# Where eight chunks of a scan pipeline do their side work, and where in the program VectorE's loop begins

## The chip, the cores and the metric

The kernel runs on one core of one Trainium2 chip. The time is that of the device, in microseconds (us), from the start to the end of one execution. All engines of the core take part: TensorE (PE in the profile; its weight loads are PEld), VectorE (DVE), ScalarE (ACT), GpSimd (POOL) and the DMA queue of SyncE (SP).

## The reference

Eight batches of 1024 rows of 256 numbers go through four residual stages: a Mamba-like selective scan (`attn_a`), a mixture of 16 experts with the top 6 chosen by a router (`ffn`), a linear attention (`attn_b`) and the mixture again. Only the first two stages are touched.

```python
def attn_a(x):                       # D_INNER 512, D_STATE 16
    xn = layernorm(x)
    x_in, z = split(xn @ in_proj)
    x_conv = silu(conv4(x_in));  Bm, Cm = split(x_conv @ x_proj)
    delta = clip(softplus(x_conv @ dt_proj), 1e-4, 10)
    for t in range(L):
        h = exp(clip(delta[t] * A, -10, 0)) * h + delta[t] * Bm[t] * x_conv[t]
        if t % 16 == 15: h = h * min(1, 10 / norm(h))
        y[t] = Cm[t] . h + D_param * x_conv[t]
    return layernorm(x + (y * silu(z)) @ out_proj)
def ffn(x):
    probs = softmax(x @ router_w + router_b); gate = top6 of probs / their sum
    return sum over e of (x @ expert_w[e]) * gate[:, e]
```

## The kernel before

A tile is 128 rows of one batch; there are 64. `step(i, k, stages)` is written once for every engine, and each engine runs its own copy for the tiles in turn; semaphores alone tie them together. In one step the scan works on tile i, the input side (normalization, projection, convolution, delta) on tiles i+1 to i+4, the output projection and its norm on tile i-1, the router on tile i-2 and the experts on tile i-3. Steps 4 to 59 are a hardware loop of 28 turns (`pipeline`, line 208), two tiles a turn (k = 0 and 1); the rest is written out.

A step has 8 chunks c of 16 rows, since the state norm is bounded every 16 rows. One chunk is a ring through four engines:

- VectorE: `scan` (L996) over 128 x 1088, two expert sums (L1078), `reduce` (L1004) of ScalarE's squares, `bound` (L1013, L1015), which scales the last column and so lets the next scan begin.
- ScalarE: squares of the last column (L438), the decays' exponentials of the next chunk (L432), the logarithm and exponential of the norm (L444, L447).
- GpSimd: `product` (L362) of chunk c-1 with C, then `inputs` (L370) of chunk c+1, which the scan of c+1 waits for. In some chunks an `extra` of one tile-wide product follows: u in chunk 1, z's gate sz (L383) in chunk 4, the convolution's output (L386) in chunk 5, the residual sum x1b (L390) in chunk 7.
- TensorE: per chunk one pair of experts (L738) and some of the projections.

Everything else is fitted between: VectorE's `start(c)` is scan and expert sums, `halfway(c)` the reduce, `end(c)` the bound. Work between halfway and end lies beside ScalarE's norm; the reduce has to wait for the squares. The 8 + 3 small steps of the router (`route_step`, `route_gate` with selp, L1068, and gate, L1070) and the output norm (o3, L1194; o4, L1197) stand there. ScalarE makes 64 decay forms zr (L423, each 128 x 128) for each tile, and the table DECAYS says how many in each chunk. In chunk 0 ScalarE makes xn (L526), which TensorE transposes (L781) ahead of `sum_states(3)` (L704). In chunk 1 TensorE turns the sums back (`sums_back`, L712), which VectorE's gating yg (L1157) waits for; the router's transposes (L720) and the input projection (L797) follow. `settle()` is a semaphore increment on VectorE and nothing else.

After tile 63 the attention and the second mixture follow, in the last third of the time.

Of the kernel before, what the change touches and what calls it, by code (L numbers as in the profile page):

```python
# [10 lines left out]
NTILES = NB * NT  # L11
# [13 lines left out]
DECAYS = (0, 6, 13, 19, 30, 37, 50, 64, 64)  # L25
# [5 lines left out]
def build(nc, dram, out):  # L31
# [3 lines left out]
    with ctx:  # L35
# [316 lines left out]
        def _(g):  # L352
# [22 lines left out]
            def extra(i, k, c, stages):  # L375
                if c == 1 and "G" in stages:
                    g.wait_ge(M["ldt"], AHEAD + i + 2)
                    g.wait_ge(M["xcv"], AHEAD + i + 2)
                    TT(u[1 - k][:], dt[:], xcv[1 - k][:], ALU.mult).then_inc(M["u"], 1)
                if c == 4 and "G" in stages:  # L380
                    g.wait_ge(M["ss"], AHEAD + i + 2)
                    g.wait_ge(M["yg"], AHEAD + (i if "B" in stages else 0))
                    TT(sz[1 - k][:], zt[:], sg[:], ALU.mult).then_inc(M["sz"], 1)  # L383
                if c == 5 and "F" in stages:
                    g.wait_ge(M["sx"], AHEAD + i + 3)
                    TT(xcv[k][:], xcv[k][:], sg[:], ALU.mult).then_inc(M["xcv"], 1)  # L386
# [21 lines left out]
        def _(a):  # L408
# [104 lines left out]
            def step(i, k, stages):  # L513
# [4 lines left out]
                for c in range(NC):  # L518
# [71 lines left out]
                    if G_ and DECAYS[c] < DECAYS[c + 1]:  # L590
                        decays(i + 1, 1 - k, DECAYS[c], DECAYS[c + 1])
                    if c == 0 and B:
                        copy_sums(i - 1, 1)
# [99 lines left out]
        def _(pe):  # L693
# [66 lines left out]
            def step(i, k, stages):  # L760
# [10 lines left out]
                for c in range(NC):  # L771
# [13 lines left out]
                    if c == 1:  # L785
                        if B:
                            sums_back(i - 1, 1)
                        if X_:
                            pe.wait_ge(M["bcv"], AHEAD + min_tiles(i + 2, stages))
                            route(i - 2, k, F1)  # L790
                        if isinstance(i, int) and i == -2:
                            pe.wait_ge(s_win, 16)
                        if F:
                            pe.wait_ge(M["xnTs"], AHEAD + (i + 3) * KD)
                            for m in range(EB):
                                for j in range(KD):
# [169 lines left out]
        def _(v):  # L966
# [98 lines left out]
            def route_gate(n, k):  # L1065

                v.wait_ge(R["router"], AHEAD + n * ROUTER + 5)
                TT(selp[:], ex[:, 0:X], rest[:, 0:X], ALU.subtract).then_inc(R["router"], 1)  # L1068
                v.wait_ge(R["router"], AHEAD + n * ROUTER + 10)
# [31 lines left out]
            def step(i, k, stages):  # L1101
# [100 lines left out]
                halfway(4)  # L1202
                if G_:
# [21 lines left out]
                router(4, 5)  # L1225
# [4 lines left out]
                router(5, 6)  # L1230
# [5 lines left out]
                router(6, 8)  # L1236
# [39 lines left out]
            V.tensor_copy(rows_of_split[96:P, :], left[96:P, :]).then_inc(s_zero, 1)  # L1276
            v.wait_ge(s_zero, 4)
# [94 lines left out]
            def slot(b, t, p):  # L1372
# [12 lines left out]
                if r is not None:  # L1385
# [9 lines left out]
                    if p == 7:  # L1395
                        route_gate(r + NTILES, r % 2)
# [65 lines left out]
```

## Time and profile before

| | |
|---|---|
| median of 3 runs | 4533.17 us (4532.49 to 4533.57) |
| the profiled execution | 4535.52 us, its span 4533.5 us |
| busy: PE, DVE, ACT, POOL | 4031.9, 3517.2, 3074.9, 2589.2 us |
| mean granted clock of TensorE | 0.959 |

The span is the time between the first and the last instruction of the profile. Busy shares are means over two stages: GpSimd has no work in the last third, and VectorE, ScalarE and GpSimd are all busy for some 86% of a stretch in the loop (1500 to 1700 us: DVE 172.40, ACT 170.57, POOL 170.91 of 200 us).

### The profile page before, as it was taken

Reading aid. Unit: us, or ns where it says so; the run is one execution under the profiler, and the core shown is the slowest. Engines: PE = TensorE matmul, PEld = TensorE weight load, DVE = VectorE, ACT = ScalarE, POOL = GpSimd, SP = SyncE. Lnnn points to the kernel's source line nnn. Section 1 sums busy time; section 2 is a strip of 40 time slices with the busy share of each in tenths; the row PEclk is TensorE's granted clock in tenths of the full one; section 3 lists DMA queues with packets and bytes.
Section 4 is the critical chain, followed back from the end, with each engine's and each line's share of the span. In section 5 each row is a group of like instructions: output and inputs, shape, how many; then the busy total and the mean of one; then the engine's idle time right before and its main releaser. Section 6 shows DMA issues by size and latency. Waiting matters only on the chain.

```text
span 4533.5 us, 71482 instructions
## 1 busy us (share of the span) xinstructions
PE 4031.9 (89%) x19008; PEld 2623.5 (58%) x19008; DVE 3517.2 (78%) x8418; ACT 3074.9 (68%) x9040; POOL 2589.2 (57%) x1284
## 2 busy tenths in 40 slices
PE   5788888888888888888888888978999999999999
PEld 5666666666666666666666666643454454454454
DVE  4788888888888888888888888984666666676576
ACT  6888888888888888888888888953333333333321
POOL 4988888888888888888888888970000000000000
PEclk8999999999999999999999999998999999999999
DMA  3111111111111111111111111110000000000000
GB/s 112 52 59 50 55 56 49 58 54 55 51 50 56 54 57 51 51 55 54 58 54 52 54 51 58 53 56 13 13 17 7 16 16 8 15 17 6 7 8 10
DMA packets 91400, 188.70 MB, mean 42 GB/s; under 512 B 15872, under 2 KB 57600, under 8 KB 90624
## 3 DMA queue, kind: packets, MB, share of 16 engines
q1 hardware_dynamic: 91136, 186.11, 12.4%
q14 instruction: 212, 1.74, 0.1%
q8 instruction: 52, 0.85, 0.1%
HBM read 168.24 MB, written 17.83 MB: 41 GB/s over the span
## 4 chain that ended last, share of the span: by engine, by line
PE 39%; ACT 22%; issue 19%; DVE 15%; POOL 4%; DVEq 1%; ACTq 0%; POOLq 0%
PE ps L738 22%; ACT zr L423 14%; DVE macc L1078 4%; PE ps L797 3%; PE ps L886 3%; PE ps L805 2%; POOL prod L362 2%; PE ps L868 2%; DVE selp L1068 1%; ACT ps_dA L432 1%; POOL hb L370 1%; PE ps_dA L886 1%; DVE xin L1189 1%; ACT sq L438 1%; PE ps_dA L868 1%
## 5 line engine op out<-in xcount | busy, mean ns | idle before, releaser
L738 PE MATMUL ps<-w_x,mxT 128*128 128x512 f32 x4096 | 1979.6, 612 | 118.7 <-DVE macc L1078 118.7
L996 DVE TENSOR_TENSOR_SCAN hb<-ps_dA,hb 128x1088 f32<-128x1088 f32 x512 | 1240.8, 2423 | 192.8 <-issue 100.8
L1078 DVE SCALAR_TENSOR_TENSOR macc<-ps,gate,macc 128x256 f32<-128x256 f32 x2048 | 979.5, 478 | 524.7 <-PE ps L738 431.9
L362 POOL TENSOR_TENSOR prod<-hb,cbc 128x1024 f32<-128x1024 f32 x512 | 1121.9, 2191 | 328.0 <-DVE hb L1015 327.5
L370 POOL TENSOR_TENSOR hb<-u,bbc 128x1024 f32<-128x1024 f32 x512 | 1200.7, 2345 | 75.1 <-POOL prod L362 70.7
L423 ACT ACTIVATE zr<-dt,aneg 128x128 f32<-128x128 f32 x4096 | 1239.9, 387 | 0.0
L738 PEld LDWEIGHTS ps<-w_x,mxT 128*128 128x128 f32 x4096 | 741.1, 195 | 835.5 <-issue 606.9
L704 PE MATMUL ps<-ident,prod 128*128 128x128 f32 x4096 | 558.9, 296 | 69.9 <-POOL prod L362 69.9
L704 PEld LDWEIGHTS ps<-ident,prod 128*128 128x128 f32 x4096 | 511.9, 153 | 89.3 <-POOL prod L362 87.1
L432 ACT ACTIVATE ps_dA<-zr 128x1024 f32<-128x1024 f32 x512 | 518.1, 1012 | 0.0
L438 ACT ACTIVATE sq<-hb 128x64 f32<-128x64 f32 x512 | 158.0, 309 | 319.9 <-DVE hb L996 319.4
L483 ACT ACTIVATE ex<-lgt,ms 128x16 f32<-128x16 f32 x128 | 39.1, 305 | 356.7 <-DVE ms L1035 356.7
L821 PEld LDWEIGHTS ps<-xin,dcw 128*128 128x128 f32 x2048 | 244.6, 196 | 21.1 <-issue 19.4
L851 PEld LDWEIGHTS ps<-xcv,w_dt 128*128 128x128 f32 x2048 | 244.3, 195 | 1.9
L821 PE MATMUL ps<-xin,dcw 128*128 128x128 f32 x2048 | 244.7, 279 | 0.0
L851 PE MATMUL ps<-xcv,w_dt 128*128 128x128 f32 x2048 | 243.4, 278 | 0.0
L797 PE MATMUL ps<-xnT,w_in 128*128 128x128 f32 x1024 | 152.6, 313 | 4.4 <-ACT xnT L548 3.3
L844 PE MATMUL ps<-xcv,w_xp 128*32 128x128 f32 x512 | 70.6, 283 | 91.9 <-POOL xcv L386 91.9
L1013 DVE SCALAR_TENSOR_TENSOR hb<-ps_dA,hb 128x64 f32<-128x64 f32 x480 | 126.5, 263 | 29.7 <-ACT ps_dA L447 29.4
L797 PEld LDWEIGHTS ps<-xnT,w_in 128*128 128x128 f32 x1024 | 146.1, 228 | 5.3 <-ACT xnT L548 3.8
L833 PEld LDWEIGHTS ps<-xnT,w_in 128*128 128x128 f32 x1024 | 124.4, 192 | 21.3 <-issue 19.5
L1015 DVE SCALAR_TENSOR_TENSOR hb<-ps_dA,hb 128x64 f32<-128x64 f32 x512 | 135.2, 264 | 0.0
(200 smaller groups left out, 4823.1 us busy)
## 6 DMA issues: line engine op xcount, KB each, us to landing
bbc<-bcd SPq DMA_DIRECT2D x128, 512.0 KB, 3.7
cbc<-bcd SPq DMA_DIRECT2D x128, 512.0 KB, 3.6
xt<-in_x SPq DMA_DIRECT2D x128, 128.0 KB, 3.8
x2d<-macc SPq DMA_DIRECT2D x64, 128.0 KB, 1.7
out_dram<-macc SPq DMA_DIRECT2D x64, 128.0 KB, 1.7
w_x<-in_w_x SPq DMA_DIRECT2D x1, 4096.0 KB, 15.5
hb<-x2d SPq DMA_DIRECT2D x32, 128.0 KB, 2.4
sz<-x2d SPq DMA_DIRECT2D x16, 128.0 KB, 2.3
```

Of the source, the lines that this page charges most:

```text
L362: TT(dst, states, cc, ALU.mult).then_inc(M["prodp"], 1)
L370: TT(hb[c % 2][:].rearrange("p (e n) s -> p e n s", e=EB)[:, :, :, 1:SL], u[k][:, :, t0:t0 + CH].rearrange("p e (n s) -> p e n s", n=1).br ...
L423: last = act(zr[k][:, s, :], dt[:, s // N, :], ACT.Relu, bias=10.0, scale=aneg[:, s:s + 1])
L432: act(dA3[:, :, 1:SL], zr[k][:, :, c * CH:(c + 1) * CH], ACT.Exp, bias=-10.0).then_inc(M["dA"], 1)
L438: act(sq[:], hb[c % 2][:, :, CH:SL].rearrange("p a b -> p (a b)"), ACT.Square).then_inc(M["sq"], 1)
L704: last = mm(YT[:, h * P:(h + 1) * P], prod[h % 2][:, n, :, :].rearrange("p e t -> p (e t)"), ident[:], start=(h % 2 == 0 and n == 0), stop ...
L738: last = mm(banks[p % len(banks)][:], mxT[k][:, j, :], w_x[:, j, p * 512:(p + 1) * 512], start=(j == 0), stop=(j == KD - 1))
L797: last = mm(F0[:, m * P:(m + 1) * P], w_in[:, j, m * P:(m + 1) * P], xnT[:, j, :], start=(j == 0), stop=(j == KD - 1))
L821: last = mm(F0[:, e * P:(e + 1) * P], dcw[:, e * TAPS + t, :], xin[:, e, t:t + P], start=False, stop=(e == EB - 1 and t == TAPS - 1))
L851: last = mm(F0[:, m * P:(m + 1) * P], w_dt[:, e, m * P:(m + 1) * P], xcv[k][:, e, :], start=False, stop=(m == EB - 1 and e == EB - 1))
L996: V.tensor_tensor_scan(states, dA, states, 0.0, ALU.mult, ALU.add).then_inc(M["scan"], 1)
L1078: STT(macc[k][:], banks[(e // 2) % len(banks)][:, (e % 2) * D:(e % 2 + 1) * D], gate[k][:, e:e + 1], macc[k][:], ALU.mult, ALU.add).then_i ...
```

## The change

Seven edits of the scan pipeline, none of which changes what is computed:

1. DECAYS: of 64 forms, chunks 0 to 7 made 6, 7, 6, 11, 7, 13, 14 and 0. Now chunks 0 to 6 make 5, 10, 5, 11, 6, 11 and 11, and chunk 7 makes the first 5 of the tile after.
2. GpSimd's sz moves from chunk 4 to chunk 3.
3. TensorE's chunk 1: the input projection first, then the router's transposes, then `sums_back`.
4. VectorE: o4 moves from chunk 3, ahead of the bound, to chunk 4, behind the reduce.
5. VectorE: router steps 2 and 3 to chunk 4, 4 and 5 to chunk 5, 6 and 7 in chunk 6.
6. VectorE: selp moves from chunk 7 to chunk 6, ahead of the bound.
7. VectorE: 72 settles ahead of the pipeline, so that the first instruction of the loop, which was VectorE's 522nd of the built program, is its 594th. The loop is 335 instructions long in both.

```diff
-DECAYS = (0, 6, 13, 19, 30, 37, 50, 64, 64)
+DECAYS = (5, 10, 20, 25, 36, 42, 53, 64)
...
-                if c == 4 and "G" in stages:
+                if c == 3 and "G" in stages:
                     g.wait_ge(M["ss"], AHEAD + i + 2)
                     g.wait_ge(M["yg"], AHEAD + (i if "B" in stages else 0))
                     TT(sz[1 - k][:], zt[:], sg[:], ALU.mult).then_inc(M["sz"], 1)
...
-                    if G_ and DECAYS[c] < DECAYS[c + 1]:
+                    if G_ and c < NC - 1:
                         decays(i + 1, 1 - k, DECAYS[c], DECAYS[c + 1])
+                    if F and c == NC - 1:
+                        decays(i + 2, k, 0, DECAYS[0])
...
                     if c == 1:
-                        if B:
-                            sums_back(i - 1, 1)
-                        if X_:
-                            pe.wait_ge(M["bcv"], AHEAD + min_tiles(i + 2, stages))
-                            route(i - 2, k, F1)
...
                             last.then_inc(M["xi"], 1)
+                        if X_:
+                            pe.wait_ge(M["bcv"], AHEAD + min_tiles(i + 2, stages))
+                            route(i - 2, k, F1)
+                        if B:
+                            sums_back(i - 1, 1)
...
+                end(3)
+
+                start(4)
+                router(0, 2)
+                halfway(4)
                 if B:
                     v.wait_ge(M["o3"], AHEAD + i)
                     STT(oo[:], oo[:], sc[:, 12:13], be_row[:], ALU.mult, ALU.add).then_inc(M["o4"], 1)
-                end(3)
-
-                start(4)
-                router(0, 2)
-                halfway(4)
+                router(2, 4)
...
-                router(6, 8)
+                router(7, 8)
+                if X_:
+                    route_selection(i - 2)
                 end(6)
...
+            for _ in range(72):
+                settle()
             v.wait_ge(s_zero, 4)
             pipeline(v, step)
```

The names are those of the buffers; line numbers of the changed kernel are 2 to 7 higher from here on (L704 is its L706, L1197 its L1207). VectorE, chunk 4 in the loop, from the reduce to the bound, before (nrs is the sum of squares, xcv the convolution's output):

```order
L1004 TENSOR_REDUCE nrs<-sq 128x4
L1205 COPY r1b<-r1a 128x1
L1208 TENSOR_SCALAR xcv<-ps 128x512
L1013 SCALAR_TENSOR_TENSOR hb<-ps_dA,hb 128x64
L1015 SCALAR_TENSOR_TENSOR hb<-ps_dA,hb 128x64
```

and now:

```order
L1006 TENSOR_REDUCE nrs<-sq 128x4
L1207 SCALAR_TENSOR_TENSOR oo<-oo,sc,be_row 128x256
L1049 TENSOR_REDUCE ms<-t 128x1
L1051 REGISTER_ALU
L1053 MATCH_REPLACE rest<-t,ex 128x18
L1211 COPY r1b<-r1a 128x1
L1214 TENSOR_SCALAR xcv<-ps 128x512
L1015 SCALAR_TENSOR_TENSOR hb<-ps_dA,hb 128x64
L1017 SCALAR_TENSOR_TENSOR hb<-ps_dA,hb 128x64
```

o4 (oo<-oo,sc,be_row) and two router steps stand between the reduce and the copy of the convolution.

TensorE, chunks 0 and 1 at the head of the loop, before:

```order
L781 MATMUL ps<-ident,xn 128x128 x2
L220 ISA
L704 MATMUL ps<-ident,prod 128x128 x16
L736 ISA
L738 MATMUL ps<-w_x,mxT 128x512 x2
L710 ISA
L712 MATMUL ps<-ident,yT 128x128 x2
L717 REGISTER_ALU
L718 REGISTER_ALU
L720 MATMUL ps<-ident,mxn 128x128 x2
L794 ISA
L797 MATMUL ps<-xnT,w_in 128x128 x8
```

and now:

```order
L783 MATMUL ps<-ident,xn 128x128 x2
L220 ISA
L706 MATMUL ps<-ident,prod 128x128 x16
L738 ISA
L740 MATMUL ps<-w_x,mxT 128x512 x2
L791 ISA
L794 MATMUL ps<-xnT,w_in 128x128 x8
L719 REGISTER_ALU
L720 REGISTER_ALU
L722 MATMUL ps<-ident,mxn 128x128 x2
L712 ISA
L714 MATMUL ps<-ident,yT 128x128 x2
```

The two transposes of yT, on which VectorE's yg waits, stand behind the input projection (xnT, w_in) and the router's (mxn), where they stood ahead of both.

ScalarE, from chunk 7 into chunk 0 of the next tile, before:

```order
L584 ACTIVATE sg<-sg 128x512
L587 ACTIVATE dt<-sg 128x512
L476 ISA
L589 ISA
L478 ISA
L479 ACTIVATE macc<-x1b,ms 128x256
L526 ACTIVATE xn<-xt,sc 128x256
L437 REGISTER_ALU
L438 ACTIVATE sq<-hb 128x64
```

and now:

```order
L584 ACTIVATE sg<-sg 128x512
L587 ACTIVATE dt<-sg 128x512
L476 ISA
L589 ISA
L478 ISA
L479 ACTIVATE macc<-x1b,ms 128x256
L423 ACTIVATE zr<-dt,aneg 128x128 x5
L526 ACTIVATE xn<-xt,sc 128x256
L437 REGISTER_ALU
L438 ACTIVATE sq<-hb 128x64
```

Five decay forms stand ahead of xn, which TensorE waits for.

## Rows read from the trace of the kernel before

**Rows 1.** The page, part 5 (out<-in, count, busy us, mean ns, idle before, its releaser)

```profile
L996 DVE TENSOR_TENSOR_SCAN hb<-ps_dA,hb 128x1088 f32<-128x1088 f32 x512 | 1240.8, 2423 | 192.8 <-issue 100.8
```

**Rows 2.** Timeline of VectorE around one turn of the loop (start us, us, operation)

```profile
1543.09 2.42 DVE L996 TENSOR_TENSOR_SCAN hb<-ps_dA,hb 128x1088 f32<-128x1088 f32 x1 [0.45 <-POOL hb L370]
...
1547.11 1.07 DVE L1068 TENSOR_TENSOR selp<-ex,rest 128x16 f32<-128x16 f32 x1
...
1552.93 2.42 DVE L996 TENSOR_TENSOR_SCAN hb<-ps_dA,hb 128x1088 f32<-128x1088 f32 x1 [3.98 <-issue]
```

**Rows 3.** The page, part 3 (queue: packets, MB, share of 16 engines)

```profile
q14 instruction: 212, 1.74, 0.1%
```

**Rows 4.** DMA queues, one whole turn of the loop, 1548.6 to 1643.4 us

```profile
q14 instruction: 5, 0.04, 0.1%
```

**Rows 5.** DMA queues, the stretch in which VectorE stands, 1549 to 1552.6 us

```profile
q14 instruction: 1, 0.01, 0.5%
```

**Rows 6.** DMA queues, 1571 to 1572.2 us

```profile
q14 instruction: 1, 0.01, 1.6%
```

**Rows 7.** VectorE's waits, 1459 to 2866 us (total us, times, longest)

```profile
DVE oo L1167 <- PE ps L805: 20.1, 30, 0.8
DVE macc L1078 <- PE ps L738: 17.3, 18, 1.5
```

**Rows 8.** Timeline of TensorE, chunks 0 and 1 of two tiles

```profile
1506.67 3.63 PE L704 MATMUL ps<-ident,prod 128*128 128x128 f32 x16 [0.88 <-POOL prod L362]
...
1512.24 0.44 PE L712 MATMUL ps<-ident,yT 128*128 128x128 f32 x2 [0.23 <-ACT yT L453]
...
1513.03 1.95 PE L797 MATMUL ps<-xnT,w_in 128*128 128x128 f32 x16
...
1561.96 3.29 PE L797 MATMUL ps<-xnT,w_in 128*128 128x128 f32 x16
```

**Rows 9.** Windows: busy us of each engine, granted clock, DMA share, GB/s

```profile
1561.00:1565.00 4.00, 3.87 (x20) 3.64 (x21) 3.27 (x6) 3.95 (x13) 4.00 (x3) 0.57 0.00 0
```

**Rows 10.** Timeline of VectorE, one tile

```profile
1504.27 2.42 DVE L996 TENSOR_TENSOR_SCAN hb<-ps_dA,hb 128x1088 f32<-128x1088 f32 x1
...
1513.25 0.69 DVE L1157 TENSOR_TENSOR sg<-ps,sz 128x512 f32<-128x512 f32 x1
...
1514.57 2.42 DVE L996 TENSOR_TENSOR_SCAN hb<-ps_dA,hb 128x1088 f32<-128x1088 f32 x1
...
1520.36 2.42 DVE L996 TENSOR_TENSOR_SCAN hb<-ps_dA,hb 128x1088 f32<-128x1088 f32 x1
...
1525.04 0.50 DVE L1194 SCALAR_TENSOR_TENSOR oo<-oo,mv,ga_row 128x256 f32<-128x256 f32 x1
...
1526.37 2.42 DVE L996 TENSOR_TENSOR_SCAN hb<-ps_dA,hb 128x1088 f32<-128x1088 f32 x1
...
1529.90 0.22 DVE L1004 TENSOR_REDUCE nrs<-sq 128x4 f32<-128x64 f32 x1
...
1531.30 2.42 DVE L996 TENSOR_TENSOR_SCAN hb<-ps_dA,hb 128x1088 f32<-128x1088 f32 x1 [0.18 <-POOL hb L370]
...
1537.20 2.42 DVE L996 TENSOR_TENSOR_SCAN hb<-ps_dA,hb 128x1088 f32<-128x1088 f32 x1 [0.74 <-POOL hb L370]
```

**Rows 11.** Timeline of GpSimd, chunks 3 and 4 of that tile

```profile
1522.91 2.34 POOL L370 TENSOR_TENSOR hb<-u,bbc 128x1024 f32<-128x1024 f32 x1 [0.17 <-POOL prod L362]
1526.49 2.20 POOL L362 TENSOR_TENSOR prod<-hb,cbc 128x1024 f32<-128x1024 f32 x1 [1.24 <-DVE hb L1015]
...
1531.16 1.29 POOL L383 TENSOR_TENSOR sz<-zt,sg 128x512 f32<-128x512 f32 x1
```

**Rows 12.** Timeline of VectorE, an early tile

```profile
124.15 1.04 DVE L1194 SCALAR_TENSOR_TENSOR oo<-oo,mv,ga_row 128x256 f32<-128x256 f32 x1
```

**Rows 13.** Timeline of GpSimd, the same moment

```profile
122.58 2.33 POOL L370 TENSOR_TENSOR hb<-u,bbc 128x1024 f32<-128x1024 f32 x1 [0.17 <-POOL prod L362]
```

**Rows 14.** Timeline of ScalarE, chunk 6

```profile
1541.94 4.19 ACT L423 ACTIVATE zr<-dt,aneg 128x128 f32<-128x128 f32 x14
```

More of the change, by code:

```diff
@@ L1063, in route_step, with route_selection, route_gate @@
                     TS(ms[:, 12:13], ms[:, 5:6], ms[:, 8:9], 1e-10, ALU.mult, ALU.mult).then_inc(R["router"], 1)
-            def route_gate(n, k):
+            def route_selection(n):
                 v.wait_ge(R["router"], AHEAD + n * ROUTER + 5)
                 TT(selp[:], ex[:, 0:X], rest[:, 0:X], ALU.subtract).then_inc(R["router"], 1)
+            def route_gate(n, k):
                 v.wait_ge(R["router"], AHEAD + n * ROUTER + 10)
@@ L1194, in step @@
                     STT(oo[:], oo[:], mv[:, 2, 0:1], ga_row[:], ALU.subtract, ALU.mult).then_inc(M["o3"], 1)
-                if B:
-                    v.wait_ge(M["o3"], AHEAD + i)
-                    STT(oo[:], oo[:], sc[:, 12:13], be_row[:], ALU.mult, ALU.add).then_inc(M["o4"], 1)
                 end(3)
@@ L1202, in step @@
                 halfway(4)
+                if B:
+                    v.wait_ge(M["o3"], AHEAD + i)
+                    STT(oo[:], oo[:], sc[:, 12:13], be_row[:], ALU.mult, ALU.add).then_inc(M["o4"], 1)
+                router(2, 4)
                 if G_:
@@ L1211, in step @@
                 start(5)
-                router(2, 3)
+                router(4, 5)
                 halfway(5)
-                router(3, 4)
+                router(5, 6)
                 if F:
@@ L1224, in step @@
                 start(6)
-                router(4, 5)
                 if L_:
@@ L1229, in step @@
                     V.bn_aggr(mv[:, 0, :], st[:, 0, :]).then_inc(M["mv1"], 1)
-                router(5, 6)
+                router(6, 7)
                 if L_:
@@ L1395, in slot @@
                     if p == 7:
+                        route_selection(r + NTILES)
                         route_gate(r + NTILES, r % 2)
```

## The prediction, made before the kernel was run

> **What bounds the kernel now.** I read the page's groups first. VectorE's scan has the largest group on the ring, and of the 192.8 us that VectorE stood ahead of a scan, 100.8 us have no releaser, only "issue" [rows 1]. The timeline puts them in one place: at the turn of the loop, between chunk 7 of one tile and chunk 0 of the next, where the scan begins after 3.98 us in which VectorE waits for nobody [rows 2]. 100.8 us over the loop's 27 turns backwards are 3.7 us each. The DMA queues say what it is. In one whole turn the queue that carries instructions moves 5 packets of 8 KB [rows 4], one of them while VectorE stands [rows 5]. How many instructions a packet holds can be estimated from the whole run: that queue moved 212 packets [rows 3], of which the loop's 28 turns make 140; the 72 left carried the programs of VectorE and ScalarE, 5700 and 3177 instructions as built, so 120 to 130 each, and I take blocks of 128. A loop of 335 that fetches five such blocks a turn does not stay in its buffer.
>
> For the ring itself I took the starts of the scans of one tile [rows 10]: chunks 0 and 1 together 10.30 us, chunk 2 5.79, chunk 3 6.01, chunk 4 4.93, chunk 5 5.90, and chunk 6 5.89 [rows 2, 10]. Chunk 4 is near the floor of the ring: scan 2.42 us, two expert sums, reduce, ScalarE's exponentials and norm, bound. Chunks 5 and 6 end on GpSimd: the scan of chunk 6 waits 0.74 us for `inputs` [rows 10], since sz, 1.29 us, stands ahead of the next product [rows 11], while in chunk 3 GpSimd has 1.24 us to spare [rows 11]. So the tile is bound by VectorE in chunks 2 and 3, by GpSimd in 5 and 6, and once every two tiles by a fetch of instructions.
>
> **Edit 7, the turn of the loop.** How many blocks a loop of 335 touches depends on how much of its first block is left at its start. Up to 78 left it touches four: the first piece, 128, 128 and a last piece; with 79 or more, three. Five packets in a turn fit four blocks and the one behind them, fetched ahead, of which one is more than the buffer keeps, so that each turn throws out what the next needs. Where the pieces lie can be read from the third packet: it falls between 1571 and 1572.2 us [rows 6], 18 to 19 us behind the scan of chunk 0 [rows 2]. The scan of chunk 3 starts 16.1 us behind it in the tile of [rows 10] and a little over 1 us later in a tile after the turn (next part), and it is the 61st instruction of the loop. So the first piece is 61 to 70. Starting 72 places later the loop runs into the next block and its first piece is 61 to 70 less 72 plus 128, that is 117 to 126; it touches three blocks. ScalarE's loop is nearly as long (321), and none of the five packets is its own, so such a loop can stay in place. I take the whole stall as gone: 27 x 3.7 = -100 us. The bound on the other side is 0.
>
> The Trainium skill (Runtime: NRT & Kernel Launch, Instruction fetch mechanics) has it that an engine holds two blocks of 256 instructions and that a taken branch out of them forces a fetch. The trace agrees on the stall and shows packets of 8 KB, not 16. By the page's blocks the loop lies in two blocks before and after, the one behind them evicts the first in both, and the stall would stay; this is the fourth case below.
>
> **What the stall drags along.** After it TensorE has idled, its granted clock is 0.57 in 1561 to 1565 us [rows 9], that is 1.2 GHz for most of it, and the input projection takes 3.29 us instead of 1.95 [rows 8]. VectorE then waits for the experts: 17.3 us in 15 turns [rows 7], 1.15 each, 32 us over 28. I take -32, bounded by 0.
>
> **The lock between VectorE and GpSimd.** selp reads two tiles of 16 numbers from SBUF and takes 1.07 us [rows 2]. o3, also with two SBUF inputs, takes 0.50 us in the loop [rows 10], and 1.04 us in an early tile [rows 12], where GpSimd's `inputs` runs from 122.58 for 2.33 us [rows 13]: it ends at 125.19, 0.28 us behind GpSimd, which is the time of its own 256 columns. So an operation of this kind waits until GpSimd's running one has ended. The same rule stands in the Trainium skill (SBUF — State Buffer, Who interferes with whom): whichever instruction starts first has the shared ports until it ends. It speaks against edits 4 and 6. By it o4 would lose the whole of `inputs`; by the free price of o4, the 0.5 us it takes now, the edit would cost nothing.
>
> **Edits 2 and 4, chunks 3 and 4 (10.94 us now).** Without o4 chunk 3 ends 0.5 us earlier, at 5.5. sz fills GpSimd's spare 1.24 us; it ends about 6.45 us after chunk 3's scan began (hb ends at 4.89 [rows 11], o3 takes the port for 0.28, sz 1.29), so the product starts there, and `inputs` of chunk 5 at 6.45 + 2.20 + 0.17 = 8.8 to 9.0, until about 11.2. o4 is ready when the reduce of chunk 4 is done: 5.5 + 3.53 + 0.22 = 9.2 [rows 10]. Should it have to wait, it ends at 11.5, and two router steps and the convolution's copy behind it need 1.5 until the scan of chunk 5 at 13.0: +2.0 us. Should it be ready ahead of `inputs`, in GpSimd's gap of 0.17 us or before it, `inputs` is what is delayed and the scan starts at 11.9: +1.0. Without any lock it would start at 11.0: 0. The moments lie within 0.3 us of each other, less than I can place them. I take +1.0 and keep 0 and +2.0. Queued behind o4 on VectorE are the copy that ScalarE's silu waits for, and the bound, which GpSimd's product and the next scan wait for.
>
> **Chunk 5.** GpSimd has no sz ahead of it. VectorE has one small step more and two fewer ahead of the bound. What is left is VectorE's own 5.15 us: 5.90 less the 0.74 us wait. -0.7, bounded by 0.
>
> **Edit 6, chunks 6 and 7.** In chunk 6 selp comes 4.0 us into the chunk (in the middle of `inputs`, which the convolution's output, 1.3 us in chunk 5, pushes back). It waits for its end, then bound and three small forms follow: +0.9, bounded by 0 if GpSimd is as much ahead. Chunk 7 loses selp's 1.07 us, of which the floor of the ring gives back 0.7.
>
> **Edits 1 and 3, chunks 0 to 2.** A decay form costs 4.19 / 14 = 0.30 us [rows 14]; five ahead of xn make it 1.5 us later, of which about half is covered by TensorE's wait for the last product. On TensorE `sums_back` stood at 1512.24 and ended 0.4 later [rows 8]; behind 1.95 us of projection and 0.4 of router transposes it ends about 1514.7 at best, while yg began at 1513.25 [rows 10]. Chunk 1 is then 1.1 to 1.8 us longer. Chunk 2 gives back the 0.67 us (20.1 in 30 tiles [rows 7]) for which VectorE waited for the output projection. I take +1.1; the ends are 0 (TensorE's clock stays up in chunk 0, where 3.63 us of `sum_states` [rows 8] are at half speed) and +1.3. The other decay shares cost nothing: ScalarE has gaps in each chunk, and 64 forms stay 64. Router steps 4 to 7 are moved between chunks at 0.2 us each, inside the figures above.
>
> **72 settles.** They stand on the first tile's path. No row shows one; between nothing and 72 of GpSimd's gaps of 0.17 us from a semaphore to the next operation [rows 11], 12 us, I take +4, since an increment waits for nobody.
>
> **The sum.** Per tile +1.1 + 1.0 - 0.7 + 0.9 - 0.7 = +1.6 us, for 61 tiles with all stages +98. With -100, -32 and +4: -30 on the profiled execution's 4535.5 us (its span of 4533.5 and 2.0 around it), 4506. That execution lies 2.4 us above the median, so I say 4504.
>
> **Rivals.**
> 1. *As summed*, 0.48: the fetch goes, the rest gives three quarters of it back. Its own range is 4450 to 4524 for the most part, and a little beyond.
> 2. *o4 waits for GpSimd's whole `inputs`* (slower): +2.0 instead of +1.0, which over 61 tiles makes 4565. It decides if o4 is ready later than the start of `inputs`; the rows put it 0.2 us behind. For it: the waits of [rows 12, 13]. Against: 0.2 us is little. It turns the sign from +1.5 on. 0.27.
> 3. *GpSimd's spare time is used and the ring closes up*, 0.18: nothing lost in chunks 0 to 4, the gains of 5 and 7 kept and the +0.9 of chunk 6 paid, 0.5 us less per tile: 4535 - 132 + 4 - 30 = 4377; with half of one cost paid, some 4410. For it: 1.24 us idle in chunk 3 against 0.74 waited in chunk 5.
> 4. *The fetch stays* (blocks twice as large, or a place that touches four blocks again), 0.07: 4504 + 132 = 4636.
>
> Within 0.2% (9 us) nothing can be told from no change by a measurement of this kernel. Faster: most of case 1 and all of 3, 0.56. Same: 0.08, the upper edge of 1 and the lower of 2. Slower: 0.36, the rest of 2 and case 4. Range 4400 to 4590.
>
> **What would show each step.** Instruction packets in a turn of the loop: 5 now, none then; idle ahead of a scan with "issue" as releaser: near 0 instead of 100.8 us. TensorE's projection at 1.95 us in both tiles of a turn. o4's duration: 0.48 where it is free, over 1 us if it waits; the scan of chunk 5 10.9, 11.9 or 13.0 us behind that of chunk 3. selp in chunk 6 over 1 us, and no wait for it in chunk 7. yg behind `sums_back` with a wait of over 1 us. The forecast is wrong if the packets stay, or if o4's wait and chunk 1's wait come out together at their upper ends (slower), or both at nothing (near 4400).

## The result, and the profile after

The changed kernel takes 4467.22 us (median of 4 runs, 4466.72 to 4468.37); the kernel before took 4533.37 beside it (4 runs, 4532.49 to 4537.38). The ratio is 0.9853, with a 95% interval of 0.9836 to 0.9870: 66 us faster. The forecast was 4504 us, 29 faster. The direction was right, and so was the end of the stall at the turn of the loop. 4467 lies in the range, but the gain is more than twice what I had forecast, and two errors of opposite sign stand behind it. The profiled execution has a span of 4465.1 us. In two of the experiments below one execution took 6379 us (e2) and 5495 us (e3), with a lower clock of TensorE than the others, and the ratios leave them out.

The page of the changed kernel, parts 5 and 3, gives the answers to [rows 1] and [rows 3] (line 998 is line 996 of the kernel before):

```profile
L998 DVE TENSOR_TENSOR_SCAN hb<-ps_dA,hb 128x1088 f32<-128x1088 f32 x512 | 1240.1, 2422 | 36.3 <-POOL hb L370 30.8
...
q14 instruction: 78, 0.63, 0.0%
```

The 100.8 us of "issue" ahead of the scans are gone and 134 packets with them. 27 turns of 5 would be 135. In a stretch longer than a whole turn, 1530 to 1625 us, the DMA queues have this single row, where [rows 4] had five packets of instructions:

```profile
q1 hardware_dynamic: 2176, 5.01, 16.7%
```

One tile on VectorE, chunks 3 to 7, its scans and the forms that were moved (o3 is line 1199, o4 line 1207, selp line 1070; it answers to [rows 10] and [rows 2]):

```profile
1491.93 2.42 DVE L998 TENSOR_TENSOR_SCAN hb<-ps_dA,hb 128x1088 f32<-128x1088 f32 x1
1496.71 0.48 DVE L1199 SCALAR_TENSOR_TENSOR oo<-oo,mv,ga_row 128x256 f32<-128x256 f32 x1
1497.50 2.42 DVE L998 TENSOR_TENSOR_SCAN hb<-ps_dA,hb 128x1088 f32<-128x1088 f32 x1
1501.16 2.10 DVE L1207 SCALAR_TENSOR_TENSOR oo<-oo,sc,be_row 128x256 f32<-128x256 f32 x1
1504.45 2.42 DVE L998 TENSOR_TENSOR_SCAN hb<-ps_dA,hb 128x1088 f32<-128x1088 f32 x1
1509.43 2.42 DVE L998 TENSOR_TENSOR_SCAN hb<-ps_dA,hb 128x1088 f32<-128x1088 f32 x1
1513.25 2.01 DVE L1070 TENSOR_TENSOR selp<-ex,rest 128x16 f32<-128x16 f32 x1
1516.15 2.42 DVE L998 TENSOR_TENSOR_SCAN hb<-ps_dA,hb 128x1088 f32<-128x1088 f32 x1
1521.30 2.41 DVE L998 TENSOR_TENSOR_SCAN hb<-ps_dA,hb 128x1088 f32<-128x1088 f32 x1
```

and GpSimd beside it:

```profile
1500.64 2.33 POOL L370 TENSOR_TENSOR hb<-u,bbc 128x1024 f32<-128x1024 f32 x1 [0.17 <-POOL prod L362]
...
1512.89 2.34 POOL L370 TENSOR_TENSOR hb<-u,bbc 128x1024 f32<-128x1024 f32 x1 [0.17 <-POOL prod L362]
```

o4 comes 0.52 us after `inputs` has begun (1500.64 to 1502.97) and ends at 1503.26, 0.29 us behind it; selp begins 0.36 us after it and ends with it. That is the lock of [rows 12, 13], once with 128 x 256 elements and once with 16 columns.

o3 shows the same from both sides. GpSimd's sz in that tile and in the next, then VectorE's o3 and o4 in the next:

```profile
1496.78 1.55 POOL L383 TENSOR_TENSOR sz<-zt,sg 128x512 f32<-128x512 f32 x1
...
1541.68 1.26 POOL L383 TENSOR_TENSOR sz<-zt,sg 128x512 f32<-128x512 f32 x1
```

```profile
1541.88 1.35 DVE L1199 SCALAR_TENSOR_TENSOR oo<-oo,mv,ga_row 128x256 f32<-128x256 f32 x1
...
1547.20 1.43 DVE L1207 SCALAR_TENSOR_TENSOR oo<-oo,sc,be_row 128x256 f32<-128x256 f32 x1
```

In the first tile o3 begins 0.07 us ahead of sz: o3 takes 0.48 us, and sz 1.55. In the second it begins 0.20 us behind sz: sz takes 1.26, and o3 1.35, to 0.29 us behind the end of sz. Of the 56 tiles in the loop 23 are of the first kind and 33 of the second.

In the first tile the scan of chunk 5 comes 12.52 us behind that of chunk 3, between my middle case (11.9) and the full one (13.0).

For the comparison of kernels I use one measure throughout: the mean distance from one scan's start to the next, by chunk, over the tiles 4 to 59, all in the loop, worked out from the starts of the scans in each trace.

```
us, mean of 56 tiles        chunks 0-2  3-5    6-7    tile
before                       16.65     16.86  13.43  46.93
e1, settles alone            16.63     16.91  11.74  45.28
e2, 40 settles               16.84     16.85  13.45  47.13
e10, 120 settles             17.01     16.86  13.42  47.29
changed kernel               16.21     17.60  11.85  45.66
e3, without its settles      16.14     17.61  13.50  47.25
e4, o4 back in chunk 3       16.09     16.93  11.85  44.87
e5, TensorE's order back     15.93     17.52  11.85  45.29
e6, decay forms back         16.00     17.64  11.85  45.49
e7, selection back           15.97     17.62  11.73  45.32
e8, z's product back         15.99     16.86  11.85  44.70
e9, e1 + edits 2 and 4       16.59     17.32  11.73  45.65
e11, e8 + e5 + e7            16.00     16.86  11.73  44.59
e12, e11 + e6                16.58     16.86  11.74  45.18
e13, e1 + edit 3             15.85     16.90  11.74  44.49
e14, e1 + edit 1             16.00     16.90  11.73  44.63
e15, e1 + edits 1 and 3      15.87     16.90  11.73  44.50
```

Read so: the turn's stall is 1.65 us a tile, all of it in chunk 7 (before to e1), and all other edits together cost 0.38 us a tile (e1 to changed), where I had charged 1.6.

### The profile page after: what moved, and what is told of

Read it like the earlier page. It is cut to its first block, busy times and chain, and to the rows that moved or that the text cites. A ratio compares the mean times of both kernels' runs of the same rounds, so it can differ in the third digit from the quotient of the medians.

```text
span 4465.1 us, 71554 instructions
## 1 busy us (share of the span) xinstructions
PE 3949.8 (88%) x19008; PEld 2583.5 (58%) x19008; DVE 3659.5 (82%) x8418; ACT 3088.2 (69%) x9040; POOL 2599.0 (58%) x1284
## 4 chain that ended last, share of the span: by engine, by line
PE 44%; issue 23%; DVE 16%; POOL 13%; ACT 2%; DVEq 1%; POOLq 0%; ACTq 0%
PE ps L740 24%; POOL prod L362 7%; DVE macc L1083 6%; PE ps L853 5%; POOL hb L370 3%; PE ps L888 3%; PE ps L870 2%; POOL xcv L386 2%; PE ps L706 2%; PE ps L846 1%; POOL u L379 1%; ACT zr L423 1%; PE ps L794 1%; PE ps_dA L888 1%; DVE xin L1194 1%
## 5 line engine op out<-in xcount | busy, mean ns | idle before, releaser
L706 PE MATMUL ps<-ident,prod 128*128 128x128 f32 x4096 | 522.8, 284 | 8.6 <-POOL prod L362 8.6
L706 PEld LDWEIGHTS ps<-ident,prod 128*128 128x128 f32 x4096 | 485.5, 147 | 13.0 <-POOL prod L362 11.3
L783 PE MATMUL ps<-ident,xn 128*128 128x128 f32 x128 | 29.4, 313 | 170.4 <-ACT xn L526 170.4
L794 PEld LDWEIGHTS ps<-xnT,w_in 128*128 128x128 f32 x1024 | 129.6, 199 | 32.9 <-issue 20.1
L783 PEld LDWEIGHTS ps<-ident,xn 128*128 128x128 f32 x128 | 13.3, 146 | 219.9 <-ACT xn L526 112.9
L835 PEld LDWEIGHTS ps<-xnT,w_in 128*128 128x128 f32 x1024 | 124.4, 192 | 21.3 <-issue 19.5
L888 PE MATMUL ps<-zr,prod 128*128 128x512 f32 x288 | 134.5, 593 | 0.0
L1017 DVE SCALAR_TENSOR_TENSOR hb<-ps_dA,hb 128x64 f32<-128x64 f32 x512 | 133.6, 261 | 0.0
```

Source lines behind the costliest of these rows:

```text
L706: last = mm(YT[:, h * P:(h + 1) * P], prod[h % 2][:, n, :, :].rearrange("p e t -> p (e t)"), ident[:], start=(h % 2 == 0 and n == 0), stop ...
L888: last = mm(QUAD[s % 4][:], w_a[:, w, kk, j * P:(j + 1) * P], xTa[:, kk, g * TG:(g + 1) * TG], start=(kk == 0), stop=(kk == KD - 1))
```

## The experiments

Each time is a median, each ratio is to the kernel before run beside it (4535 to 4537 us).

**e1: the settles alone.** The kernel before with

```diff
+            for _ in range(72):
+                settle()
             v.wait_ge(s_zero, 4)
             pipeline(v, step)
```

> The kernel before with the 72 settles alone (loop at place 594). Theory A (the turn gave what was forecast, 100 + 32 - 4 = 128 us, and my sum charged the moved forms too much: +98 forecast, about +60 in truth): 4533 - 128 = 4405 us, range 4395 to 4415, faster than the changed kernel by about 60. Theory B (the forms cost the forecast +98 and the turn was worth more than 128, by the 37 us that are missing): about 4368 us. Theory C (the moved forms removed the turn's stall or cost nothing, and the settles do little): 4460 to 4537 us. VectorE's instruction queue: 5 packets in a whole turn now; none by A and B.

Measured: 4443.52 us, ratio 0.9797 (0.9781 to 0.9814): 92 us faster than before, and 24 faster than the changed kernel. That is in none of the three ranges: the turn gave less than the 128 I had put on it, and the other edits cost far less than 98. Both steps were off, with opposite signs.

**e2: 40 settles, and e10: 120.** As e1, with `range(40)` and `range(120)`.

> The kernel before with 40 settles (loop at place 562, its first 8 KB piece cut so that it still touches four pieces). Theory A (what counts is over how many 8 KB pieces the loop reaches: three are held, four are not): stall and 5 packets a turn stay, 4533 + 2 = 4535 us. Rival (any shift to a later place, or the distance from the start, helps in part): between 4405 and 4500 us. Control for e1.

> The kernel before with 120 settles: loop's first instruction at place 642, 48 later than e1's, cut so that four 8 KB pieces hold a part of the loop again. Theory A (pieces, not distance): 5 packets a turn and the wait are back, 4535 + 8 to 10 = 4540 to 4552 us. Rival (later is better, or 594 passed some mark): 4443 to 4452 us.

Measured: 4547.04 us, 1.0025 (1.0015 to 1.0035), and 4564.57 us, 1.0059 (1.0042 to 1.0075). The pages, parts 3 and 5, of e2, e10 and e1 in this order:

```profile
q14 instruction: 212, 1.74, 0.1%
...
L996 DVE TENSOR_TENSOR_SCAN hb<-ps_dA,hb 128x1088 f32<-128x1088 f32 x512 | 1240.7, 2423 | 193.1 <-issue 101.6
```

```profile
q14 instruction: 214, 1.75, 0.1%
...
L996 DVE TENSOR_TENSOR_SCAN hb<-ps_dA,hb 128x1088 f32<-128x1088 f32 x512 | 1240.8, 2423 | 199.5 <-issue 109.1
```

```profile
q14 instruction: 77, 0.63, 0.0%
...
L996 DVE TENSOR_TENSOR_SCAN hb<-ps_dA,hb 128x1088 f32<-128x1088 f32 x512 | 1240.7, 2423 | 98.2 <-POOL hb L370 88.8
```

At 562 and 642 the five packets a turn stay, at 594 they are gone. So it is the place against the 8 KB pieces, not the distance. With pieces of 128 instructions the four places together put a boundary of two pieces between 563 and 592; my estimate, 522 and 61 to 70 more, lies at 583 to 592. e2 is 12 us and e10 29 us above the kernel before, e10 also 12 above the top of theory A's range. The first scan of e10 begins 11.6 us later (74.0 against 62.4 us; in e2 it is 4.6 us), and chunk 2 takes 6.70 us on average against 6.34, 20 us in 56 tiles: TensorE's clock falls in chunk 1 in more of its tiles (20 against 14).

**e3: the changed kernel without its settles.**

```diff
-            for _ in range(72):
-                settle()
```

> The changed kernel without its settles (loop's first instruction back at place 522, the forms as changed). Theory A: 5 packets a turn and the wait of 3.7 us of VectorE are back, 4467 + 128 = 4595 us at the price forecast (+100 if the stall drags nothing along: 4563), slower than the kernel before by 30 to 62 us. Theory B: 4467 + 165 = 4632. Theory C (forms did it): 4463 to 4475.

Measured: 4546.94 us, 1.0028 (1.0015 to 1.0040), 80 above the changed kernel, where theory A had 96 to 128 and the others lie farther off. The queue's 212 packets and 89.9 us of "issue" are back. So without the turn's gain, the other edits are a loss of 0.3% on the kernel before.

**e4: o4 back in chunk 3.** In the changed kernel the two lines of o4 stand ahead of `end(3)` again, instead of behind `halfway(4)`.

> The changed kernel with the norm's last form (o4, the scale by gamma) back in chunk 3, so that no plain form of VectorE meets GpSimd's inputs in chunk 4. Theory A (o4 waits for the end of inputs, and the scan behind it comes late; chunks 3 and 4 lost 1.66 us a tile, o4's wait of 1.44 to 2.10 less its own 0.48 being most of it): chunk 4 from 6.5 back to about 5.6, chunk 3 from 6.05 to about 6.5, net -0.4 to -1.2 us a tile, 4467 - 25 to 73 = 4394 to 4442 us. Rival (in chunk 3 o4 meets the product where o3 already does, and the loss moves there whole): 4463 to 4475 us.

**e8: z's product back in chunk 4**, o4 staying there:

```diff
-                if c == 3 and "G" in stages:
+                if c == 4 and "G" in stages:
```

> The changed kernel with z's product (GpSimd, 1.55 us where it shares, about 0.95 else) back in chunk 4, o4 staying there. Theory A (GpSimd's extra operation lengthens its own chunk by what it takes, wherever it is, and o4 in chunk 4 then comes to share with both): chunk 3 shorter by 0.5 to 1.1, chunk 4 longer by 0.8 to 1.5 us, sum 0 to +0.5 us a tile, 4467 to 4500 us. Rival (z's product in chunk 3 is what costs, by o3's 1.29 us wait behind it): 4400 to 4440 us.

**e9: the two edits alone on e1**, z's product in chunk 3 and o4 in chunk 4.

> e1's kernel (the one before with the 72 settles) with two edits alone: z's product in chunk 3 and o4 in chunk 4. e4 and e8, each with both in one chunk, were 48 and 58 us faster than the changed kernel. Theory A (the two in different chunks cost 0.7 us a tile: each chunk in which GpSimd shares with a scaled form, or carries its extra product, grows by about 1.1 us over 5.0 plus the router's): chunks 3 to 5 go from 16.90 to 17.5 or more, 4443.5 + 37 to 61 = 4480 to 4504 us. Rival (the price is from the router's steps that were moved with them): 4438 to 4452 us.

Measured: e4 4419.05 us (0.9747, 0.9731 to 0.9763), as theory A had it; e8 4409.36 us (0.9723, 0.9707 to 0.9739); e9 4476.98 us (0.9872, 0.9855 to 0.9888), 33 above e1, between the two ranges and nearer to theory A's. In e4 chunk 3 rose by 0.88 and chunk 4 fell by 1.57 us. For e8 the time is the rival's, and my theory did not hold: chunk 3 fell by 0.49 and chunk 4 fell too, by 0.26. Nor does z's product take 0.95 us anywhere: alone it takes 1.28. The groups of o3, o4 and z's product from 300 to 2800 us, first of the changed kernel:

```profile
L1207 DVE SCALAR_TENSOR_TENSOR oo<-oo,sc,be_row 128x256 f32<-128x256 f32 x55 | 94.3, 1715 | 0.0
L383 POOL TENSOR_TENSOR sz<-zt,sg 128x512 f32<-128x512 f32 x55 | 75.9, 1380 | 0.0
L1199 DVE SCALAR_TENSOR_TENSOR oo<-oo,mv,ga_row 128x256 f32<-128x256 f32 x55 | 53.2, 967 | 2.0
```

then of e8:

```profile
L383 POOL TENSOR_TENSOR sz<-zt,sg 128x512 f32<-128x512 f32 x56 | 82.0, 1464 | 0.0
L1207 DVE SCALAR_TENSOR_TENSOR oo<-oo,sc,be_row 128x256 f32<-128x256 f32 x56 | 81.3, 1451 | 0.0
L1199 DVE SCALAR_TENSOR_TENSOR oo<-oo,mv,ga_row 128x256 f32<-128x256 f32 x56 | 27.2, 485 | 2.0
```

and of e1, where none of the three meets another:

```profile
L383 POOL TENSOR_TENSOR sz<-zt,sg 128x512 f32<-128x512 f32 x55 | 70.2, 1276 | 0.0
L1194 DVE SCALAR_TENSOR_TENSOR oo<-oo,mv,ga_row 128x256 f32<-128x256 f32 x56 | 27.2, 485 | 2.0
L1197 DVE SCALAR_TENSOR_TENSOR oo<-oo,sc,be_row 128x256 f32<-128x256 f32 x55 | 26.7, 485 | 2.0
```

Chunks 3 to 5 make a table of four: 16.91 us with z's product in chunk 4 and o4 in chunk 3 (e1), 16.93 with both in chunk 3 (e4), 16.86 with both in chunk 4 (e8), and 17.60 with z's product in chunk 3 and o4 in chunk 4 (the changed kernel; e9 17.32). Either move alone costs nothing, and the two together do (e4, e8 and the changed kernel have the router's steps moved too). The traces show how. In e1, e4 and e8 GpSimd's `inputs` in chunk 4 ends 4.81 to 4.83 us behind that chunk's scan; with z's product ahead of it in chunk 3 and o4 in chunk 4 it ends 5.44 us behind it (e9, mean of 56 tiles; 5.09 in the changed kernel, whose chunk 3 is 0.41 us longer than e9's), and o4, which has to wait for that end, takes 2.06 us, where it takes 1.45 in e8.

The rival of this, that o3 waits behind z's product in chunk 3, explains little. It does so in 33 of the changed kernel's 56 tiles (0.97 us on average against 0.49), but these tiles take 17.67 us in chunks 3 to 5, and the 23 others 17.50. In e9 o3 takes over 0.7 us in 4 tiles only. What is left between 17.32 and 17.50 is by the router's steps or by another edit; that was not tried by itself. (The profiled execution of e9, from which its row is, has a span of 4466 us, 11 below the median of its executions, so that row is rather too low.)

**e7: the selection back in chunk 7.** The call of `route_selection` moves from the end of chunk 6 to ahead of `route_gate` in chunk 7.

> The changed kernel with the router's selection (selp and what goes with it) back in chunk 7. In chunk 6 selp took 2.00 us, to the end of GpSimd's inputs; in chunk 7 of the kernel before it took 1.07. Theory A (it meets GpSimd in either chunk, and each costs the like): chunk 6 -0.83, chunk 7 +0.72, 4467 - 7 = 4460 us, range 4448 to 4470. Rival (chunk 7 has slack now that forms left it, so that the 0.83 is gained whole): 4467 - 50 = 4417 us.

Measured: 4447.60 us (0.9805, 0.9789 to 0.9822), 20 faster and just below theory A's range. Of its 0.34 us a tile only 0.11 lie in chunks 6 and 7, which is theory A's trade. The other 0.24 lie in chunks 0 to 2 and were not forecast. The trace shows where: in 23 tiles of either kernel TensorE's clock falls in chunk 0, and chunk 1 of these tiles takes 6.13 us in e7 and 6.64 in the changed kernel.

**e5: TensorE's old order in chunk 1, e6: the old decay forms**, both on the changed kernel.

```diff
 # e5, ahead of the input projection again instead of behind it
+                        if B:
+                            sums_back(i - 1, 1)
+                        if X_:
+                            pe.wait_ge(M["bcv"], AHEAD + min_tiles(i + 2, stages))
+                            route(i - 2, k, F1)
 # e6
-DECAYS = (5, 10, 20, 25, 36, 42, 53, 64)
+DECAYS = (0, 6, 13, 19, 30, 37, 50, 64)
```

> The changed kernel with TensorE's old order in chunk 1 (router's products behind the sums for the norm, that is right after chunk 1's transposes). Chunks 0 to 2 turned out 0.42 us a tile cheaper than in e1, where I had charged +1.1. Theory A (the sums are needed by yg in chunk 1, and the order is what makes it wait 0.5 to 1.15 us in the changed kernel): chunk 1 gains 0.3 to 0.7 us a tile and the rest is ScalarE's, 4467 - 18 to 43 = 4424 to 4449 us. Rival (the order gains, by letting the sums find product and transposes ready): slower by 0.3 to 0.8 us a tile, 4485 to 4516 us.

> The changed kernel with the decay forms (ScalarE's zr and its exponentials' inputs) spread as before, none of them in chunk 7. Theory A (the even spread ends the waits of VectorE for ScalarE's sq and decays in chunks 1 and 2, 0.39 + 0.22 us in e1's chunk 1; the chunks 0 to 2 gain by it what they gained): chunks 1 and 2 longer by 0.4 to 0.8 us a tile, 4467 + 25 to 50 = 4492 to 4517 us. Rival (the spread is indifferent and the gain of chunks 0 to 2 is TensorE's order or z's product): 4458 to 4476 us. Against both, the +1.1 that I charged (xn late by the forms put in chunk 7): 4400 us.

Measured: e5 4448.45 us (0.9807, 0.9791 to 0.9823), 19 faster, in theory A's range; e6 4459.24 us (0.9831, 0.9814 to 0.9847), 8 faster, the rival's range. Undone one at a time, either edit looks like a small loss. Yet with both in place chunks 0 to 2 were 0.42 us shorter than in e1. The next runs show why.

**e11: z's product, selection and order back; e12: the decay forms too.**

> The changed kernel with three edits undone: z's product back in chunk 4, selection back in chunk 7, TensorE's old order in chunk 1 (o4 stays in chunk 4, the router's other steps and the even decay forms stay). From e8's 44.70 us a tile: selection -0.1, chunk 1's slow stretches gone -0.3 to -0.4: 44.2 to 44.3 us, 4409 - 24 to 30 = 4380 to 4385 us; range 4370 to 4410 (the order gives nothing once z's product is in chunk 4: 4403).

> e11 with the old decay forms too, so that of the changed kernel only the settles, o4 in chunk 4 and the router's steps of chunks 4 to 6 are left. Theory A (the even spread gives nothing, e6: -8 us when undone): 4375 to 4387 us, within 8 us below e11. Rival (in e1 VectorE waits 0.39 + 0.22 us for ScalarE in chunk 1 and TensorE has more slow stretches, 56 against 23; the even spread is what ended both): 4400 to 4430 us.

Measured: e11 4407.97 us (0.9712, 0.9696 to 0.9728), e12 4441.76 us (0.9791, 0.9774 to 0.9807). e11 is hardly below e8 (4409) and not at the 4380 to 4385 that I had worked out: beside z's product in chunk 4 the old order gives nothing. e12 is the rival's case and beyond its range. Beside the old order the even decay forms are worth 34 us; beside the new one they cost 8. e6 had misled me, since it undid one of two edits whose gains overlap.

**e13: edit 3 alone on e1; e14: edit 1 alone; e15: both.**

> e1's kernel with TensorE's new order in chunk 1 alone (router's products before the sums for the norm). Theory A (each of edits 1 and 3, alone, takes away the late oo of chunk 2; in e6, the new order with the old forms, chunks 0 to 2 took 16.00 us against 16.63 in e1): 4443 - 0.6 x 61 = 4407 us, range 4400 to 4415. Rival (my charge: sums_back comes later, yg with it, +0.3 to +1.1 us a tile): 4460 to 4510 us. No effect would be 4443.

> e1's kernel with the even decay forms alone (five of the next tile's in chunk 7). Theory A (e11 against e12: -34 us): 4410 us, range 4402 to 4420, chunks 0 to 2 at 16.0 us. Rival (my charge: xn late by the forms in chunk 7, +0.3 to +1.1 us a tile): 4460 to 4510 us.

> e1's kernel with edits 1 and 3 together and nothing else of the change. Theory A (they take away the same delay, so they don't add up, and together they bring back a wait of yg in the tiles with a slow stretch of TensorE: chunks 0 to 2 at 16.0 to 16.2 us as in e8 and the changed kernel): 4407 to 4420 us, not below the better of e13 and e14. Rival (they add up): 4370 to 4380 us.

Measured: e13 4397.63 us (0.9697, 0.9680 to 0.9713), e14 4407.31 us (0.9718, 0.9702 to 0.9734), e15 4399.88 us (0.9699, 0.9683 to 0.9715). Beside e1, edit 3 alone is worth 46 us, edit 1 alone 36 and both 44. They don't add up, as theory A had it; e13 lies 2 us below its range and e15 7 us. **e13 is the fastest kernel of the study**, 70 us below the changed one (e15 can't be told from it). VectorE's groups from 300 to 2800 us show what goes and what comes; first e1 (macc is the experts' sum, sg the form yg, oo the output's sum):

```profile
L1078 DVE SCALAR_TENSOR_TENSOR macc<-ps,gate,macc 128x256 f32<-128x256 f32 x884 | 418.3, 473 | 54.8 <-PE ps L738 38.7
...
L1157 DVE TENSOR_TENSOR sg<-ps,sz 128x512 f32<-128x512 f32 x55 | 38.1, 692 | 3.9
...
L1167 DVE SCALAR_TENSOR_TENSOR oo<-xt,r1b,ps 128x256 f32<-128x256 f32 x56 | 26.9, 481 | 37.8 <-PE ps L805 37.8
```

then e13:

```profile
L1078 DVE SCALAR_TENSOR_TENSOR macc<-ps,gate,macc 128x256 f32<-128x256 f32 x898 | 423.5, 472 | 20.5 <-PE ps L738 3.1 <-DVE macc L1078 0.5
...
L1157 DVE TENSOR_TENSOR sg<-ps,sz 128x512 f32<-128x512 f32 x56 | 38.7, 692 | 32.1 <-PE ps L712 32.1
...
L1167 DVE SCALAR_TENSOR_TENSOR oo<-xt,r1b,ps 128x256 f32<-128x256 f32 x56 | 26.4, 471 | 0.0
```

and the changed kernel:

```profile
L1083 DVE SCALAR_TENSOR_TENSOR macc<-ps,gate,macc 128x256 f32<-128x256 f32 x875 | 412.7, 472 | 37.3 <-PE ps L740 21.6
...
L1162 DVE TENSOR_TENSOR sg<-ps,sz 128x512 f32<-128x512 f32 x54 | 37.3, 692 | 41.7 <-PE ps L714 41.7
L1172 DVE SCALAR_TENSOR_TENSOR oo<-xt,r1b,ps 128x256 f32<-128x256 f32 x55 | 26.1, 474 | 0.0
```

In the new order yg waits 0.57 us a tile (32.1 / 56), as I had said in kind; but oo's 0.68 and most of macc's 0.69 are gone. In e14 oo still waits 0.63 us a tile, so that edit 1 does not take away the late oo, as theory A said; there ScalarE's yT comes earlier (TensorE's transposes of it begin 2.73 us behind the scan of chunk 1, 3.02 in e1), and the clock falls in chunk 1 of 3 tiles in place of 15. For edit 3 TensorE shows the reason. Its timeline in a tile of e1 (scan of chunk 1 at 1515.20):

```profile
1518.23 0.44 PE L712 MATMUL ps<-ident,yT 128*128 128x128 f32 x2 [2.00 <-ACT yT L453]
1518.80 0.64 PE L720 MATMUL ps<-ident,mxn 128*128 128x128 f32 x2
1519.23 3.41 PE L797 MATMUL ps<-xnT,w_in 128*128 128x128 f32 x16
1522.48 1.88 PE L738 MATMUL ps<-w_x,mxT 128*128 128x512 f32 x4
1524.20 0.27 PE L803 MATMUL ps<-split,ones 128*128 128x256 bf16 x1
1524.31 1.89 PE L805 MATMUL ps<-w_out,sg 128*128 128x256 f32 x8
```

and in one of e13 (scan of chunk 1 at 1491.77):

```profile
1492.79 2.05 PE L792 MATMUL ps<-xnT,w_in 128*128 128x128 f32 x16
1495.37 0.43 PE L720 MATMUL ps<-ident,mxn 128*128 128x128 f32 x2 [0.53 <-ACT mxn L467]
1495.64 0.38 PE L712 MATMUL ps<-ident,yT 128*128 128x128 f32 x2
1495.86 1.88 PE L738 MATMUL ps<-w_x,mxT 128*128 128x512 f32 x4
1497.58 0.27 PE L803 MATMUL ps<-split,ones 128*128 128x256 bf16 x1
1497.69 1.89 PE L805 MATMUL ps<-w_out,sg 128*128 128x256 f32 x8
```

In the old order TensorE stands 2.00 us for ScalarE's copy yT, until 1518.23, with the projection queued behind it, although its input xnT is written at 1516.16; then the projection delays the experts' products and the output projection, which comes 9.11 us behind the scan of chunk 1. In the new order the projection fills that gap and the output projection comes after 5.92 us. (Means of 56 tiles: 7.87 and 5.97 us.) The windows of e1 also show the clock: 1.00 in 1510 to 1516 us, then, after the 2 us in which TensorE stood, 0.55 (1.2 GHz for nearly all of it) while the projection runs, and that is why it took 3.41 us and not 1.95:

```profile
1518.80:1522.60 3.80, 3.80 (x19) 3.80 (x20) 3.36 (x5) 3.75 (x13) 3.80 (x3) 0.55 0.00 0
1510.00:1516.00 6.00, 3.89 (x22) 2.58 (x22) 5.49 (x12) 3.66 (x11) 5.13 (x3) 1.00 0.61 196
```

That tile of e1 is one of 15. In these TensorE waits 1.88 to 2.05 us for yT, the clock falls behind the wait, and chunk 2 takes 7.43 us. In the other 41 the clock has fallen in chunk 0 already, TensorE comes late to the transposes and waits 0.31 us on average, and chunk 2 takes 5.92. In e13 the clock falls in no chunk 1, and in chunk 0 of 8 tiles only; in the other 48 chunk 2 takes 5.44. Of the 0.93 us a tile that chunk 2 gains, some 0.40 (15 x 1.51 / 56) are thus the falls in chunk 1, and the rest the earlier output projection and the fewer falls in chunk 0.

Over 300 to 2800 us the mean granted clock is 0.96 in e1, 0.97 in e14, 0.98 in the changed kernel and 0.99 in e13 and e15. By the records of the clock in tiles 4 to 59, it falls in 61 places in the kernel before, in 56 in e1, 15 of them in chunk 1; in 43 in e14, 3 in chunk 1; in 8 in e13 and e15, and in 23 in the changed kernel, all in chunk 0.

## Why the prediction was right and wrong, step by step

**"Edits 1 and 3, chunks 0 to 2": the step that failed.** I took +1.1 us a tile, with 0 as the lowest end; it measured -0.42 (16.21 against 16.63), below my lower bound: chunk 0 +0.08, chunk 1 +0.33, chunk 2 -0.83, where I had chunk 1 at +1.1 to +1.8 and chunk 2 at -0.67. In 61 tiles the error is 93 us. Two parts were right: xn is late (TensorE's wait for it, lines 781 and 783, went from 85.0 to 170.4 us in the whole run, 1.4 us a tile), and yg waits (0.77 us a tile, 41.7 / 54). Wrong was what they cost. I placed `sums_back` behind the projection by adding the projection's 1.95 us to a tile in which TensorE had waited 0.23 us for yT [rows 8]. In e1 it waits 0.31 us on average in the 41 tiles in whose chunk 0 the clock falls, and 1.88 to 2.05 us in the 15 others, and there the projection fills the wait. In the new order the clock falls in chunk 0 of 8 tiles (e13; 23 in the changed kernel), so that most tiles are of that kind, and the transposes of yT come 0.9 us later on average (e13, 3.92 against 3.02 us behind the scan), not 2.4. And I priced nothing for what the new order takes off the experts and the output projection, except the 0.67 us of oo. In e13 chunk 1 is longer by 0.15 us (5.50 against 5.35): VectorE's waits in it are 0.90 us (0.58 for yg, 0.32 for ScalarE) where in e1 they were 0.63 (0.31 for the experts, 0.32 for ScalarE). A reason for a gain below zero stood in the rows: the projection at 3.29 us [rows 8] and the experts that were late 18 times [rows 7], which I took for the stall's doing.

**"What the stall drags along": wrong.** I took -32 us. e1 removed the stall, and TensorE's clock still falls in 56 places against 61: chunk 2 takes 6.32 us on average against 6.34, and VectorE's wait for the experts in it 0.39 us against 0.42. The late experts belong to chunks 0 and 1 and not to the turn; edit 3 alone and edit 1 alone each take away most of that wait in chunk 2 (0.08 us are left in e14).

**"Edit 7, the turn of the loop": right, somewhat too large.** No packets, no "issue", as said, and e2 and e10 confirm the pieces. The Trainium skill (Runtime: NRT & Kernel Launch, Instruction fetch mechanics) speaks of two blocks of 256 instructions. Counted from the program's start, the loop lies in the same two such blocks at 522, 562, 594 and 642, and the stall could not go and come as it did. No other start of such blocks helps: for 562 to reach into a third, a boundary has to lie at 563 to 640, for 642 one at 643 to 720, and these are no multiple of 256 apart. The measurement decides. e1 gives -1.65 us a tile, -92 us over 56 tiles, where I took -100. From the other side e3 is 80 us slower, the settles' own cost already taken off.

**"72 settles": +4 taken, about +6 measured**: e1's first scan begins 6.0 us later than before (68.4 and 62.4 us). In the other kernels with 72 settles it begins at 68.2 to 70.9 us.

**"Edits 2 and 4, chunks 3 and 4" and "Chunk 5"**: +1.0 - 0.7 = +0.3 us taken, +0.69 measured (chunks 3 and 4 +1.61, chunk 5 -0.92): 24 us too little. o4 waits for the end of `inputs` in every tile, as in rival 2, and takes 1.42 to 2.12 us. The Trainium skill (SBUF — State Buffer, Who interferes with whom) has it that whoever issues first keeps the shared ports for the whole instruction; the trace agrees, for o4 and `inputs`, and for o3 and z's product in both orders. What I had not seen is that o4 is dear only because z's product in chunk 3 makes that end late: with z's product in chunk 4 the move of o4 costs nothing (e8).

**"Edit 6, chunks 6 and 7": right.** +0.83 and -0.72 against +0.9 and -0.7.

**Smaller slips.** The chance of slower, 0.36, is more than the whole of cases 2 and 4, 0.34, of which it was said to consist. And in the tile behind the turn the scan of chunk 3 comes 1.8 us later than in the tile of [rows 10], not a little over 1 us (17.87 against 16.09 us behind that of chunk 0); the packet still falls behind it, and the place of the pieces holds.

Together: the prediction's -128 for the turn with its settles was -92 in e1, 36 too much; its +98 for the other edits was +24. The two errors, 36 and 74 us, have opposite signs and differ by 38, and 4504 less 38 is 4466: that the time lies near the forecast is in part luck. Of rival 2 the mechanism came true at a smaller price, and of rival 3, the ring that closes up, e13 shows that 4397 us was there, but by another way than the one I gave.

What is open: why the clock of TensorE falls in fewer places with the new order. The runs show that it goes with less waiting for yT in chunk 1, but no run changed the waiting alone, and the wait by itself does not decide: in e14 TensorE waits 1.58 to 1.72 us for yT in 16 tiles, and the clock falls in chunk 1 of 3 of them. Also open is why the selection's place (e7) changes chunk 1 in the tiles where the clock falls in chunk 0.

## What to carry to other kernels

When an in-order engine's steps are swapped, look at what it waits for at the step that is overtaken, over all tiles and at either level of the clock: a ready product put ahead of a late operand costs only what is longer than the wait, and everything behind it comes earlier. Two edits whose gains overlap look worthless when each is undone alone; test them from the other side too, each alone on the plain kernel. Two moves that cost nothing alone can be dear together, if one makes late what the other waits for; test them together and apart. And when instruction packets come in every turn of a loop, count the pieces of code that the loop touches before looking for the stall at its turn anywhere else.

## What the runs showed of the hardware

A loop of 335 instructions of VectorE has five 8 KB packets and a wait of 3.0 to 4.1 us in every turn (89.9 to 109.1 us over 27) when it begins at 522, 562 or 642, and none at 594: 92 us of 4535 for 72 instructions that do nothing.

Where a form of VectorE with two inputs in SBUF and a product of GpSimd meet, the one that starts later waits for the other's end, and its recorded duration holds the wait. It holds for a form of 16 columns as for one of 256: selp takes 1.08 us in chunk 7 (e1) and 2.01 in chunk 6. And it holds both ways, for starts 0.06 to 0.5 us apart: o3 takes 1.05 to 1.36 us and z's product 1.26 to 1.29 in the 33 tiles in which z's product starts first, and 0.48 and 1.49 to 1.56 in the 23 in which o3 does.
